# GPS layer kernel: POOL waits for landed rows at every fourth batch, residual rows behind the sums, comparisons in three buffers, index tables in 96 rows

## What is computed

```python
xn  = layernorm(x)
msg = relu(xn[src] + edge_attr)                  # one row of 256 for each edge
agg = zeros_like(xn).at[dst].add(msg)            # segment sum into the nodes
gnn = node_mlp(xn + agg)                         # batch norm, two matmuls, graph norm, relu
q, k, v = split(xn @ W_qkv + b_qkv)              # the mixer, linear in the number of nodes
kv  = einsum("nc,nd->cd", normalised(k * k), v)
mix = (v + normalised(q * q) @ kv / sqrt(N)) @ W_out + b_out
x   = x + gnn + mix
out = x + mixture_of_8_experts(layernorm(x), top 2)
```

## Time and profile before

| what | us |
|---|---|
| median of 3 runs (lowest, highest) | 2675.56 (2665.64, 2679.72) |
| the profiled execution's own time | 2669.44 |
| its span, first to last instruction | 2667.6 |
| busy in the span: PE, DVE, ACT, POOL | 1859.1, 1231.2, 805.7, 1164.5 |
| mean granted TensorE clock | 0.822 of full speed |

### The profile page before, as it was taken

One profiled execution on the slowest core, in us unless ns is written; L12 is line 12 of the kernel. 1 busy time (PEld: TensorE's weight loads), 2 busy tenths in 40 slices (PEclk: granted clock), 3 DMA queues, 4 the chain that ended last, 5 costly groups with the idle time before them and its releaser, 6 DMA issues. The chain is left out here.

```text
span 2667.6 us, 36477 instructions
## 1 busy us (share of the span) xinstructions
PE 1859.1 (70%) x10110; PEld 1470.0 (55%) x10111; DVE 1231.2 (46%) x3939; ACT 805.7 (30%) x1670; POOL 1164.5 (44%) x1123
## 2 busy tenths in 40 slices
PE   2166565656656777777786789673419999999993
PEld 2144343434434444444454678562418888888883
DVE  3444443544544544454544444553315544454441
ACT  2222221212211222222222246541214444444441
POOL 0366665656765655555563000134761222222221
PEclk9577777777777878888887899656659999999997
DMA  4455544555554655565553800467942222222234
GB/s 161 147 171 172 189 156 158 185 176 170 179 180 150 204 178 180 180 196 179 185 186 118 250 1 0 127 196 171 265 110 41 45 43 47 48 46 43 46 48 112
DMA packets 186297, 362.49 MB, mean 136 GB/s; under 512 B 41332, under 2 KB 135537, under 8 KB 172763
## 3 DMA queue, kind: packets, MB, share of 16 engines
q0 software_dynamic: 74144, 155.59, 22.7%
q1 hardware_dynamic: 99264, 199.22, 22.5%
q10 hardware_dynamic: 12795, 6.60, 1.2%
HBM read 292.91 MB, written 74.69 MB: 138 GB/s over the span
## 5 line engine op out<-in xcount | busy, mean ns | idle before, releaser
L187 POOL DMA_INDIRECT gathered<-xn_rows,src_table x832 | 829.6, 997 | 516.1 <-DVE edge_attr L623 262.9
L795 PE MATMUL bank<-edge_attr,dst_select 128*128 128x256 f32 x1664 | 543.9, 494 | 375.6 <-issue 365.8
L795 PEld LDWEIGHTS bank<-edge_attr,dst_select 128*128 128x128 f32 x1664 | 416.1, 256 | 500.5 <-issue 410.9
L1816 PE MATMUL bank<-rowsT_parts,expert_weights 128*128 128x256 f16 x3564 | 409.0, 273 | 10.2 <-issue 6.4
L1816 PEld LDWEIGHTS bank<-rowsT_parts,expert_weights 128*128 x3564 | 346.5, 98 | 59.2 <-issue 18.2
L1783 POOL DMA_INDIRECT output_rows<-expert_out,token_index x108 | 167.4, 1550 | 475.0 <-DVE token_index L1936 446.5
L623 DVE TENSOR_TENSOR edge_attr<-gathered,edge_attr 128x256 f32<-128x256 f32 x832 | 288.2, 419 | 101.2 <-DMA gathered<-xn_rows,src_table 71.4
L720 ACT ACTIVATE edge_attr<-edge_attr 128x2048 f32<-128x2048 f32 x104 | 198.6, 1910 | 387.3 <-DVE edge_attr L623 288.5
L1829 PE MATMUL bank<-expert_weights,gated_parts 128*128 x1836 | 209.3, 273 | 0.6 <-DVE gated_parts L1931 0.6
L1923 DVE SCALAR_TENSOR_TENSOR gated<-bank,silu 128x512 f32<-128x512 f32 x216 | 120.7, 559 | 163.0 <-ACT silu L1861 162.0
L1829 PEld LDWEIGHTS bank<-expert_weights,gated_parts 128*128 128x128 f16 x1836 | 179.5, 98 | 21.7 <-issue 0.9
(11 more groups left out here) (274 smaller groups left out, 2160.6 us busy)
## 6 DMA issues: line engine op xcount, KB each, us to landing
edge_attr<-in_edge_attr SPq DMA_DIRECT2D x104, 1024.0 KB
dispatched_rows<-empty_row SPq DMA_DIRECT2D x2, 7410.0 KB, 36.0
rows<-dispatched_rows SPq DMA_DIRECT2D x55, 260.0 KB
gathered<-xn_rows,src_table POOLq DMA_INDIRECT x832
raw_weights<-in_L_ffn_w SPq DMA_DIRECT2D x16, 640.0 KB
out<-output_rows SPq DMA_DIRECT2D x1, 6250.0 KB, 22.2
rows_in<-xn_rows SPq DMA_DIRECT2D x48, 128.0 KB
rows_in<-in_x SPq DMA_DIRECT2D x48, 128.0 KB
```

Of the source, the lines that this page charges most:

```text
L187: pool.indirect_dma_start(out=k.GA[h][:, e, :], out_offset=None, in_=k.xn_d[:, :], in_offset=bass.IndirectOffsetOnAxis(ap=k.src[:, b, e:e ...
L795: last = pe.matmul(WINP[b % 2][:, 0:C], SEL[b % 2][:, e, :], EA[b % 3][:, e, :], start=e == 0, stop=e == EK - 1)
L1816: last = pe.matmul(bank[:, jj * TT:(jj + 1) * TT], w(e, wp, at + b * step, 128), X16[h][:, xp, b, :], start=n == 0, stop=n == 3 * CB - 1)
```

## The change

It has five parts.

1. POOL, ahead of the gathers of every fourth batch (b = 4, 8, ... 100), also waits for a new semaphore `add_begun`, which DVE increments with the first add of a batch. The value b is reached when the first add of batch b - 1 has been made, and that add itself waits for all gathers of batch b - 1.
2. DVE makes the comparisons of batch b + 1 between the adds of batch b, one comparison ahead of each add, into three buffers instead of two. Those of batch 0 come before the loop. The wait for `win_full` moves with them, now ahead of the first of these pairs.
3. `residual` moves behind `add` and `into_tiles`.
4. The index tables are loaded as 96 rows, 7 rows and 1 row instead of 103 rows and 1. That is one DMA more on SP's queue for each table.
5. The layernorm stage issues the gathers of batch 0 alone, and the edge stage those of batch 1.

Besides, six waits of PE that others imply are dropped, and the semaphore `sel_done`.

```diff
--- before.py
+++ after.py
@@ -252,10 +252,11 @@
...
                 load(n)
-            body = (NB - 1) * EB
+            body, even = (NB - 1) * EB, NB // 16 * 16
             t = lambda name: A[name]
             for to, name in ((dsti, "dst"), (srci, "src")):
-                sp.dma_start(to[0:NB - 1, :], t(name)[0:body].rearrange("(b i) -> b i", i=EB)).then_inc(tab_in, 16)
+                sp.dma_start(to[0:even, :], t(name)[0:even * EB].rearrange("(b i) -> b i", i=EB)).then_inc(tab_in, 16)
+                sp.dma_start(to[even:NB - 1, :], t(name)[even * EB:body].rearrange("(b i) -> b i", i=EB)).then_inc(tab_in, 16)
                 sp.dma_start(to[NB - 1:NB, :], t(name)[LAST:E].rearrange("(b i) -> b i", i=EB)).then_inc(tab_in, 16)
@@ -331,8 +332,7 @@
...
             pool.wait_ge(xn_st, 16 * (NG + 1))
-            for b in range(2):
-                gather(k, pool, b, b)
+            gather(k, pool, 0, 0)
 
@@ -360,7 +360,7 @@
...
             def table_floats():
-                dve.wait_ge(tab_in, 16 * 4)
+                dve.wait_ge(tab_in, 16 * 6)
                 dve.tensor_copy(dstf[:, :], dsti[:, :]).then_inc(tab_f, 1)
@@ -506,7 +506,7 @@
...
     GA, g_in = k.GA, k.g_in
-    SEL = [sb(f"dst_select{h}", [128, EK, NP], F32, st) for h in two]
+    SEL = [sb(f"dst_select{h}", [128, EK, NP], F32, st) for h in three]
     XT = [sb(f"rows_in{h}", [128, C], F32, st) for h in two]
@@ -533,8 +533,8 @@
...
     r_out = [sem(f"residual_out{h}") for h in two]
-    added, relu_done, sel_done, win_full, evac = (sem(n) for n in (
-        "edges_added", "relu_done", "select_done", "window_full", "window_added"))
+    added, relu_done, win_full, evac = (sem(n) for n in (
+        "edges_added", "relu_done", "window_full", "window_added"))
     kp_full, kb_done, k2_done, rs_done, k4_done, kv_used = (sem(n) for n in (
@@ -543,6 +543,8 @@
...
     stray_full, stray_out = sem("strays_summed"), sem("strays_copied")
+    add_begun = sem("first_edges_added")
+    RUN = 4
     P1, P2 = 1, PT + 5
@@ -601,26 +603,30 @@
...
         def _(pool):
-            for b in range(2, NB):
-                pool.wait_ge(added, b - 1)
+            for b in range(1, NB):
+                if b >= 2:
+                    pool.wait_ge(added, b - 1)
+                if b % RUN == 0:
+                    pool.wait_ge(add_begun, b)
                 gather(k, pool, b, b % 2)
...
         def _(dve):
-            def select(b):
-                h = b % 2
-                if b >= 2:
-                    dve.wait_ge(win_full, b - 1)
-                for e in range(EK):
-                    last = dve.tensor_scalar(SEL[h][:, e, :], k.iota[:, :], k.dstp[:, b, e:e + 1], None, ALU.is_equal)
-                last.then_inc(sel_done, 1)
+            def select(b, e):
+                dve.tensor_scalar(SEL[b % 3][:, e, :], k.iota[:, :], k.dstp[:, b, e:e + 1], None, ALU.is_equal)
 
...
                 dve.wait_ge(g_in[b % 2], 16 * EK * (b // 2 + 1))
+                if b > 1:
+                    dve.wait_ge(win_full, b - 1)
                 for e in range(EK):
+                    if b + 1 < NB:
+                        select(b + 1, e)
                     last = dve.tensor_tensor(ea[:, e, :], ga[:, e, :], ea[:, e, :], ALU.add)
+                    if e == 0:
+                        last.then_inc(add_begun, 1)
                 last.then_inc(added, 1)
@@ -696,13 +702,14 @@
...
 
+            for e in range(EK):
+                select(0, e)
             for b in range(NB):
-                select(b)
-                if is_tile(b - P2 - 2):
-                    residual(b - P2 - 2)
                 add(b)
...
                     into_tiles(b - 1)
+                if is_tile(b - P2 - 2):
+                    residual(b - P2 - 2)
                 if is_tile(b - P1):
@@ -787,25 +794,19 @@
...
             def scatter(b):
-                pe.wait_ge(sel_done, b + 1)
                 pe.wait_ge(relu_done, b + 1)
-                if b >= 2:
-                    pe.wait_ge(evac, b - 1)
                 for e in range(EK):
-                    last = pe.matmul(WINP[b % 2][:, 0:C], SEL[b % 2][:, e, :], EA[b % 3][:, e, :], start=e == 0, stop=e == EK - 1)
+                    last = pe.matmul(WINP[b % 2][:, 0:C], SEL[b % 3][:, e, :], EA[b % 3][:, e, :], start=e == 0, stop=e == EK - 1)
                 last.then_inc(win_full, 1)
...
                 v, h = rows_of(t), t % 2
-                if t >= 2:
-                    pe.wait_ge(kb_done, t - 1)
                 for c in range(CB):
...
                 v, h = rows_of(t), t % 2
-                pe.wait_ge(rs_done, t + 1)
                 pe.wait_ge(k4_done, t + 1)
@@ -843,8 +844,6 @@
...
                 pe.wait_ge(q2_done, t + 1)
-                if t >= 1:
-                    pe.wait_ge(q2t_done, t)
                 for c in range(CB):
@@ -854,8 +853,6 @@
...
                     pe.wait_ge(stray_out, 1)
-                if t >= 2:
-                    pe.wait_ge(r_done, t - 1)
                 for c in range(CB):
```

## The result

The changed kernel takes 2728.26 us (median of 4 runs, 2718.16 to 2734.57). The kernel before, run beside it, takes 2671.78. The ratio is 1.021, with a 95% interval of 1.017 to 1.025: slower by 2.1%. The forecast was 2705, slower. The profiled execution takes 2734.57 us at a span of 2732.8, against 2669.44 at a span of 2667.6 for the profiled one of before.

The account below looks back on a forecast made before the run. The prediction took long runs of POOL's gathers, holding back PE's signals in the edge stage, as the bound. 2669.4 - 35 + 32 + 37 = 2703.4, forecast as a median of 2705 us; range 2545 to 2738.

Parts of the forecast that it names:

- Term 1: Start: index tables spread over DMA engines and earlier gathers make batch 2 start 34.8 us earlier; -35 us.
- Term 2: First pass: the new wait makes POOL start 2.4 us later at 13 waits; +32 us, bounds 0 and 65.
- DVE resumes at T + 45.7: First pass: DVE goes on 45.7 us after the start T of a run of 32 gathers, as measured before.
- the clog: Edge stage: a long run of POOL's gathers holds back PE's signals until POOL pauses; DVE 19.8 us late once.
- rival C: Edge stage: held-back signals get through mid-run in half the cycles, POOL's waits of two lengths; 2604 us, chance 0.18.
- Term 3: Second pass: the wait makes POOL late, then 32 gathers run without pause; +37 us, bounds -45 and +60.
- the cycle of 54.6 us: Second pass: four batches with one run of 32 gathers take 54.6 us against 51.2, 3.4 us more.
- The 2.9 us until PE's signals are in: Second pass: time from POOL's stop until ACT takes PE's turn (1092.15 to 1095.07), counted in each cycle.
- The comparisons, 0: First pass: putting DVE's comparisons between its adds costs nothing and gains nothing; 0 us.
- B: Both passes: the wait for landed rows clears what holds back PE's signals; 2503 us, chance 0.16.
- D: Both passes: the new wait falls into POOL's existing 10 us pause, only the earlier start counts; 2634 us, chance 0.18.
- A: The forecast itself: earlier start outweighed by losses in both passes; 2705 us, own range 2660 to 2740, chance 0.42.

Follow-up runs that it names:

- the start alone: Kernel before with only the index tables in 96, 7 and 1 rows and batch 1 gathered in the edge stage: 2423.15 us, 0.983.
- the second measurement: The changed kernel run again, unaltered, beside the kernel before: 2709.96 us, 1.015.
- the block ahead of the adds: Changed kernel without POOL's wait and with the eight comparisons in one block before the eight adds: 2586.23 us, 0.971 of the kernel before.
- RUN = 2: Changed kernel with POOL's wait at every second batch instead of every fourth: 2603.85 us, 0.978 of the kernel before.

## Why the prediction was right, and where it was wrong

**Term 1, -35 us: right.** Batch 4 starts 35.5 us earlier. The wait for the tables was 29.1 and is gone, as the prediction had it by the Trainium skill ("DMA: Bandwidth & Descriptors", section "Why a DMA increments its semaphore by 16 and not by 1"). The trace agrees by the cast at 18.78 without a wait. Alone on an open chip the start is worth 40.4 us.

**Term 2, +32 us: wrong in size.** The twelve cycles from batch 4 to 52 cost 4.5 us more, not 12 x 2.4 = 29. The step that failed is "DVE resumes at T + 45.7" for every cycle: the waits at b = 4, 8, ... 52 are 3.2 to 7.1 us in seven cases and 9.6 to 13.0 in the six others, so the clog often let go in mid-run, rival C's mark. That the delay of 2.4 us is near the 2.8 us that the wait costs where nothing clogs is chance: there POOL issues without a break and loses its own wait of 3.1 us, which is another path than the one that was added up. On the clogging chip the mean cycle takes it up, the lower bound that the prediction kept (0, "if the phase of the cycle takes it up").

**Term 3, +37 us: the right sign and place, less than half the size.** It measured 93.3. The step that failed is the cycle of 54.6 us with one run of 32 and one pause. It measured 59.5 (655.01 / 11). The trace shows mostly runs of 24 and of 8, with a pause behind each: two waits in a cycle, 9.1 and 8.6 us in the rows above. In the whole stage there are 36 waits, not 25, from 2.6 to 23.4 us long. The 2.9 us until PE's signals are in were read from a row in which the signal is only 1.4 us late (1093.64 to 1095.07); ACT's turns come 6.5 to 19.7 us late in 12 cases after the change, and once, by 6.9, before it. So the sum priced the clog of the second pass from rows that hardly show it. And the wait costs 6.6 us a time even where nothing clogs, which is 72 of the 93 us in eleven cycles if the two chips' costs can be set side by side. The longer gathers are at most 16.6 us of the 93. How the loss divides between the clog and the lost lead was not told apart. The lower bound was given as -45, where 12 x 3.6 is 43; nothing hangs on it.

**The comparisons, 0: wrong where nothing clogs.** The step "the move of the comparisons costs nothing and gains nothing" counted DVE's own time only. The comparison and the add, in turn, make the gathers beside them 1.29 us long instead of 0.95, and putting the comparisons back where they were saves 32.8 us on an open chip. This was not isolated on a clogging chip, where the mean gather went from 997 to 1013 ns.

**The residual, and the six PE waits.** The residual's move gave little: on the clogging chip its cycles are as long as before. On open ones the start alone has 0.983, and the changed kernel without the wait and with the comparisons at the end has the same; its second pass is 15.9 us shorter (501.80 to 485.95), but the last four batches and the turn of the passes give part of that back. No run isolated the PE waits.

**The rivals.** B, "the clog goes" (2503), priced the second pass at the undisturbed loop of 11.9 us. No run had that with the wait at every fourth batch in: on an open chip too it makes a batch of the second pass 13.1 us (574.22 / 44). D, "the wait is free" (2634), had the first pass nearly right, and failed in the second. C's two kinds of wait came, without C's gain. A was the likeliest and came: 2705 against 2728. The terms add up to a rise of 34 us; 65 came between the two profiled executions, 56 between the medians and 42 in the second measurement. That it is this near is in part luck: one term was too large by 28 us, one too small by 56, and the cost of the comparisons left out.

**What stays open.** What holds the signals back, and why in some sets only. The runs show that it comes with runs of 24 to 32 gathers, is nearly absent with 16, and is nearly absent too in a first pass of hundreds of gathers with a stretched one in most batches. They do not show whether POOL must be idle, rows must have landed, or a longer gather is pause enough. What the changed kernel without its wait, and nothing else altered, does on a clogging chip was not run. Nor was the version without the wait and with the comparisons at the end, which on an open chip is as fast as the start alone (2416.22 and 2423.15 us in two sets). There the block ahead of the adds (0.971) and RUN = 2 (0.978) beat both kernels, but RUN = 2, with the comparisons at the end, loses 3.6% on an open chip. Nothing was shown to be best on both kinds.

## What to carry to other kernels

A wait that keeps one engine from running ahead can cost its whole lead: price it as the time from the release to the next landing (14.3 us here), against the period of the loop, not as the few us that it adds to one signal's path. When work is moved on DVE, look at what POOL does beside it, since its gathers can be stretched by it, here from 0.95 to 3.55 us. And time the kernel before on more than one chip, before a cure for a stall is built on one of them.

## What the runs showed that I had not expected

- The same kernel takes 2461 us on one chip and 2668 on another, 8% apart, each steady within 1%. Where it is slow, signals of PE come late while POOL issues gathers, in the kernel before by up to 19.8 us; where it is fast, none of those that I timed does.
- On an open chip, in the first pass, 112 gathers go out in a row with some 0.3 us between them, and then comes a stall of 2.3 us or more. No load of SP and no turned tile for ACT is late.
- On a clogging chip over 350 gathers went out without a wait for DVE, and almost nothing was late in that stretch.
- A gather of 0.95 us takes 1.29 beside comparisons and adds in turn, 3.55 where a block of adds follows a block of comparisons without a gap, and 0.95 where 0.46 us lie between.
- A drain on POOL, behind a gather and a memset, took 2.0 us.
